# State-space layer on one core: ten products per half dealt otherwise between GpSimd and VectorE, and its steps placed anew

## The reference

```python
def _mamba(x, W_in, conv_w, conv_b, W_xproj, W_dt, b_dt, A_log, D_param, W_out):
    xp, z = jnp.split(x @ W_in.T, 2, axis=-1)              # 384 channels each
    xc = jax.nn.silu(causal_conv(xp, conv_w, 4 taps) + conv_b)
    dt, Bt, Ct = jnp.split(xc @ W_xproj.T, [12, 28], axis=-1)   # 16 states
    dt = jax.nn.softplus(dt @ W_dt.T + b_dt)
    A = -jnp.exp(A_log)
    def step(h, inp):
        dt_t, B_t, C_t, x_t = inp
        h = jnp.exp(dt_t[..., None] * A) * h + (dt_t * x_t)[..., None] * B_t[:, None, :]
        return h, jnp.einsum('bdn,bn->bd', h, C_t)
    y = scan(step) + xc * D_param
    return (y * jax.nn.silu(z)) @ W_out.T
h = h + 0.5 * (_mamba(ln(h)) + _mamba(ln(h)[:, ::-1])[:, ::-1])
```

## Time and profile before

| | before |
| --- | --- |
| median of 3 runs | 4684.36 us (4680.06 to 4692.94) |
| profiled execution | 4681.88 us, its span 4680.0 us |
| state-space scans | from 1221 to 3772 us of the span |
| busy share: TensorE, VectorE, GpSimd, ScalarE | 86%, 66%, 62%, 60% |

### The profile page before, as it was taken

The page is one execution under the profiler, slowest core; times in us unless marked ns, Lnnn a source line. Parts: engine busy times, 40 slices in busy tenths (PEclk is TensorE's granted clock), DMA queues, the critical chain, the costliest instruction groups (busy, mean ns, idle before and its releaser), DMA issues. The chain is left out here.

```text
span 4680.0 us, 76208 instructions
## 1 busy us (share of the span) xinstructions
PE 4045.9 (86%) x23616; PEld 2763.0 (59%) x23616; DVE 3086.8 (66%) x4728; ACT 2818.8 (60%) x4976; POOL 2901.5 (62%) x1573
## 2 busy tenths in 40 slices
PE   7999986997789988988998889889888766999994
PEld 4666654664456666666666666556565644666673
DVE  5766673111498888888888888888888875111114
ACT  3555542222688787888888887878788734121221
POOL 3222211442588888898988898888989841444441
PEclk9999996998899999999999999999999888999997
DMA  1000011343233333333333333333333321343456
GB/s 35 21 20 20 20 46 55 118 117 92 79 101 100 100 99 101 91 103 99 103 95 102 99 99 101 101 100 99 101 92 102 96 67 49 108 121 109 131 167 221
DMA packets 313323, 430.59 MB, mean 92 GB/s; under 512 B 44524, under 2 KB 181564, under 8 KB 312988
## 3 DMA queue, kind: packets, MB, share of 16 engines
q1 hardware_dynamic: 281856, 352.71, 25.6%
q0 software_dynamic: 28032, 73.17, 6.2%
q10 hardware_dynamic: 3100, 0.64, 0.1%
HBM read 359.42 MB, written 41.81 MB: 86 GB/s over the span
## 5 line engine op out<-in xcount | busy, mean ns | idle before, releaser
L1894 POOL TENSOR_TENSOR m_xh<-m_xh,m_Cb 128x1536 f32<-128x1536 f32 x320 | 1127.6, 3550 | 163.6 <-DVE m_xh L1877 163.2
L1903 POOL TENSOR_TENSOR m_xh<-m_u,m_Bb 128x1536 f32<-128x1536 f32 x320 | 1130.2, 3570 | 151.8 <-PE bank L1790 119.1
L1790 PE MATMUL bank<-ident,m_xh 128*128 128x128 f32 x6144 | 866.6, 283 | 59.2 <-issue 42.1
L1790 PEld LDWEIGHTS bank<-ident,m_xh 128*128 128x128 f32 x6144 | 728.6, 145 | 230.8 <-issue 204.8
L1877 DVE TENSOR_TENSOR_SCAN m_xh<-m_xh,bank 128x512 f32<-128x512 f32 x576 | 681.3, 1208 | 153.0 <-PE bank L1840 119.6
L1859 ACT ACTIVATE bank<-m_dt,m_Ac 128x512 f32<-128x512 f32 x960 | 635.1, 682 | 235.9 <-DVE m_xh L1887 154.2
L1877 DVE TENSOR_TENSOR_SCAN bank<-bank,m_xh 128x512 f32<-128x512 f32 x576 | 688.7, 1214 | 48.8 <-ACT bank L1859 46.7
L1877 DVE TENSOR_TENSOR_SCAN m_xh<-bank,m_xh 128x512 f32<-128x512 f32 x384 | 451.2, 1208 | 106.0 <-ACT bank L1859 98.6
L1840 PE MATMUL bank<-ident,m_uB 128*128 128x128 f32 x2304 | 375.5, 287 | 151.5 <-DVE m_xh L1887 100.5
L1204 ACT ACTIVATE f1t_h<-bank,f1t_b 128x512 f32<-128x512 f32 (+1 forms) x276 | 147.9, 587 | 509.7 <-PE bank L1234 509.7
L1831 ACT ACTIVATE m_uB<-m_uT,m_BT 128x384 f32<-128x384 f32 x768 | 407.7, 603 | 25.9 <-PE bank L1840 24.1
(11 more groups left out here) (381 smaller groups left out, 7047.6 us busy)
## 6 DMA issues: line engine op xcount, KB each, us to landing
m_Cb<-BC_rows SPq DMA_DIRECT2D x512, 256.0 KB, 3.4
m_Bb<-BC_rows SPq DMA_DIRECT2D x320, 256.0 KB, 4.2
f1t_w<-f_w SPq DMA_DIRECT2D x46, 576.0 KB
m_r<-m_dt POOLq DMA_DIRECT2D x32, 768.0 KB, 8.9
f1t_w1a<-f_w SPq DMA_DIRECT2D x46, 384.0 KB
f0t_w<-f_w SPq DMA_DIRECT2D x22, 576.0 KB
f1c_yg<-rows_y SPq DMA_DIRECT2D x16, 768.0 KB, 8.2
f1t_w1b<-f_w SPq DMA_DIRECT2D x92, 96.0 KB
```

Of the source, the lines that this page charges most:

```text
L1790: mm = pe.matmul(bank[:, c, sl], xh[n % NX][:, c, sl], K.ident[:, :], is_transpose=True, start=False, stop=(d == 1 and n == NS - 1), skip_ ...
L1894: pool.tensor_tensor(v, v, Cb[n % RC][:, :].unsqueeze(1).to_broadcast([P, DC, TOK]), ALU.mult).then_inc(s_prp, 1)
L1903: pool.tensor_tensor(xh[n % NX][:, :, :], u[d][:, :, :], Bb[k % RB][:, :].unsqueeze(1).to_broadcast([P, DC, TOK]), ALU.mult).then_inc(s_dB ...
```

## The change

Two tables change and nothing else: which states GpSimd reads out, and the positions of the steps.

In half 0 GpSimd reads out states 3, 11 and 15 in place of 4, 9 and 10; in half 1 states 1 and 15 in place of 0 and 9. The number stays ten a half, and VectorE's stays six. `BY_TURN` stays. In the diff the names ending in 0 or 1 belong to the preparation of half 0 or 1, which stands in the half before it; `pe_T`, `act_uB` and `pe_D` stand in their own half.

```diff
-            "pe_BT0": 17, "act_BT0": 19, "pe_BT1": 13, "act_BT1": 14, "act_uB0": (0, 10, 15, 21, 30, 35),
-            "act_uB1": (6, 9, 16, 20, 26, 36), "pe_T0": (6, 12, 18, 22, 30, 35), "pe_T1": (2, 6, 16, 24, 31, 35),
-            "pe_uT0": (36, 42, 46), "act_uT0": (38, 44, 47), "pe_uT1": (35, 39, 42), "act_uT1": (36, 41, 43), "y": (5, 6, 9),
-            "pe_yT": (8, 9, 11), "act_yT": (10, 11, 12), "pe_D0": (10, 12, 18), "pe_D1": (0, 6, 32), "pe_out": (15, 16),
-            "out": (15, 19), "act_rows": (8, 13), "rows": (8, 13), "stats": 15, "rstd": 17, "norm": 38, "pe_zT": (40, 47),
-            "act_zT": (42, 44), "pe_x0": (0, 1, 1), "act_x0": (0, 0, 2), "pe_conv0": (1, 1, 4), "act_conv0": (5, 7, 13),
-            "pe_conv1": (3, 3, 3), "act_conv1": (1, 3, 5), "pe_gate1": (23, 25, 28, 29), "act_gate1": (27, 29, 31, 33),
-            "pe_dt0": (18, 20, 21), "act_dt0": (21, 23, 24), "pe_dt1": (17, 21, 21), "act_dt1": (17, 23, 23), "pe_pj": (9, 9),
-            "act_pj": (16, 11), "act_xc": (14, 7), "act_e": (24, 25), "act_w1": (29, 26), "act_ln": (32, 31),
-            "pe_sp0": (34, 34, 40), "act_sp0": (36, 36, 42), "u0": (35, 35, 41), "pe_sp1": (33, 34, 37), "act_sp1": (34, 35, 40),
-            "u1": (34, 36, 39),
+            "pe_BT0": 17, "act_BT0": 20, "pe_BT1": 12, "act_BT1": 14, "act_uB0": (2, 10, 15, 21, 28, 33),
+            "act_uB1": (2, 9, 16, 20, 27, 34), "pe_T0": (7, 11, 17, 23, 30, 34), "pe_T1": (2, 6, 14, 24, 31, 35),
+            "pe_uT0": (37, 47, 47), "act_uT0": (40, 43, 44), "pe_uT1": (35, 36, 45), "act_uT1": (39, 40, 43), "y": (5, 6, 9),
+            "pe_yT": (7, 10, 13), "act_yT": (11, 13, 14), "pe_D0": (11, 14, 18), "pe_D1": (8, 16, 26), "pe_out": (15, 16),
+            "out": (16, 17), "act_rows": (9, 13), "rows": (9, 13), "stats": 18, "rstd": 27, "norm": 41, "pe_zT": (43, 47),
+            "act_zT": (43, 44), "pe_x0": (1, 1, 1), "act_x0": (0, 1, 3), "pe_conv0": (1, 1, 4), "act_conv0": (6, 8, 11),
+            "pe_conv1": (0, 0, 1), "act_conv1": (0, 4, 5), "pe_gate1": (23, 27, 27, 30), "act_gate1": (26, 29, 29, 33),
+            "pe_dt0": (19, 21, 21), "act_dt0": (23, 24, 24), "pe_dt1": (18, 19, 20), "act_dt1": (20, 21, 22), "pe_pj": (9, 9),
+            "act_pj": (17, 12), "act_xc": (14, 8), "act_e": (24, 24), "act_w1": (31, 27), "act_ln": (32, 32),
+            "pe_sp0": (33, 35, 42), "act_sp0": (37, 37, 41), "u0": (36, 39, 41), "pe_sp1": (32, 33, 40), "act_sp1": (34, 36, 41),
+            "u1": (35, 35, 41),
...
-        BY_POOL = (0, 2, 4, 5, 6, 8, 9, 10, 12, 14), (0, 2, 4, 5, 6, 8, 9, 10, 12, 14)
+        BY_POOL = (0, 2, 3, 5, 6, 8, 11, 12, 14, 15), (1, 2, 4, 5, 6, 8, 10, 12, 14, 15)
```

## The result

The changed kernel takes 4607.9 us (median of 4 runs, 4606.3 to 4615.3) against 4683.3 us for the kernel before. The ratio is 0.984, with a 95% interval of 0.982 to 0.986: faster by 75 us. The forecast was 4632, its range 4592 to 4702. The profiled execution of the changed kernel took 4615.3 us, its span 4612.5, so the traces differ by 67.5 us; the rest of the 75 lies in the spread of the runs, and what follows explains the 67.5.

A forecast was written before the change was run, and what follows sets the result against it. No single engine bounds it; the limit moves between TensorE, GpSimd and ScalarE. Terms 0.4 + 3.2 + 0 + 1.4 - 1.5 = 3.5 us a group, over 15 passages 52 us: 4632 us, range 4592 to 4702.

The forecast's parts named there:

- The signs named for it: Unit 30's wait under 1 us, unit 6's 1.5 to 3, projection 2 us sooner, a group of 156 to 158.
- new small waits: Gaps from gates and transposes at new positions and later bank release: 1.5 us a group lost, bounds 0 and 3.
- Unit 0 to 24 of half 0: Start of a group: first `y` needs the same convolutions and sums either way; +0.4 us, bounds -1.5 and +1.
- Unit 24 to unit 8 of half 1: From half 0 into half 1, paced by TensorE: its queue gets shorter, 3.2 us a group won.
- two sums, a D term, two waits: TensorE, unit 24 to unit 8 of half 1: savings of 1.0, 1.0 and 1.16 us, sum 3.2.
- The wait at 1796.03: TensorE's 0.58 us wait for VectorE's read-out of state 1: goes because GpSimd now reads that state.
- The wait at 1778.44: TensorE's 0.58 us wait that hangs on `zT`: loses its cause, moving with its step.
- Unit 8 to 33 of half 1: Stretch paced by ScalarE, with the same steps in the same sum: 0 us, bounds -1 and +0.5.
- Unit 33 to the next group: End of half 1, paced by GpSimd: one 3.5 us read-out less in its chain; +1.4 us, bounds -1 and +2.
- the gain is swallowed: Rival, chance 0.17: unit 30's waits go but ScalarE or TensorE is next late; 0.4 us a group, 4678 us.
- The read-out of state 11: Rival, chance 0.13: GpSimd's half 0 chain hangs on unit 35's scan, delaying read-out 12; 1.5 us a group lost, 4707 us.
- The clock rival: Rival, chance 0.05: TensorE's clock falls from 0.97 to 0.88 in half 0's second stretch, 4.0 us longer; 4744 us.

The follow-up runs named there:

- conv_back: The changed kernel with half 1's convolutions back at their old positions, behind the last sums: 4599.4 us, ratio to before 0.981.
- mend_d: The changed kernel with the first D term of half 0 at position 13 for 11, behind state 4's transposes: 4630.9 us, ratio to before 0.989.
- mend_conv: The changed kernel with ScalarE's first copy of a convolution in half 0 at position 2 for 0: 4610.3 us, ratio to before 0.984.
- mend_t8: The changed kernel with state 8's transposes in half 1 at position 22 for 24: 4595.6 us, ratio to before 0.980.
- places_only: The changed kernel's positions with the states dealt as before in both halves: 4719.3 us, ratio to before 1.007.
- half0_states: The changed kernel's positions, half 0's states dealt anew and half 1's as before: 4658.6 us, ratio to before 0.994.
- states_only: The kernel before with only the states dealt anew, all positions old: 4733.7 us, ratio to before 1.010.
- half1_states: The changed kernel's positions, half 1's states dealt anew and half 0's as before: 4653.1 us, ratio to before 0.993.
- dterm_back: The changed kernel with half 1's D terms back at positions 0, 6 and 32 for 8, 16 and 26: 4628.2 us, ratio to before 0.987.

## Why the prediction was right, and where it was not

The forecast was right in sign and nearly in size: 3.5 us a group for a measured 3.8 in the loop. The signs named for it came: 0.18 us before unit 30, 1.70 before unit 6 of half 1, the projection 3 us sooner after state 8's first transpose, a group of 156.4. That the sum is off by only 0.3 is partly luck. The first part came out 2.4 lower than forecast, and the reserve of 1.5 for new small waits and 0.5, 0.2 and 0.5 in the other parts made up for it. Nor did the sum foresee that either half of the change alone would cost time.

*Unit 0 to 24 of half 0: +0.4 forecast, -2.0 measured.* This step failed, and beyond its bound of -1.5. It held that the first `y` waits for the same work either way, which is so: `y` waits 0.18 for 0.80. But it looked at `y` alone, and it put TensorE's clock at nothing. ScalarE's first convolution copy now stands ahead of the decays of units 1 and 2, and the D term stands between state 4's transposes while it waits for ScalarE's copy of `yT`. TensorE in the changed kernel:

```profile
1705.27 0.66 PE L1840 MATMUL bank<-ident,m_uB 128*128 128x128 f32 x4 [1.41 <-ACT m_uB L1831]
...
1706.45 1.59 PE L1780 MATMUL bank<-m_dgD,m_xc 128*128 128x128 f32 x8 [0.53 <-ACT m_r L1803]
...
1708.69 1.06 PE L1840 MATMUL bank<-ident,m_uB 128*128 128x128 f32 x4
```

The state 4 transposes start at 1705.27, and the second set only at 1708.69. But the runs that undo one of these places each win back only 0.4 to 0.7 of the 2.0 us here (`conv_back`, `mend_d`, `mend_conv`). The rest goes with the clock: the lower level, 0.50, takes 5.5 us of this stretch on average, for 0.5 in the kernel before. `mend_d` shows its price within one execution, in the second and third group:

```profile
1529.60:1574.80 45.20, 42.34 (x223) 30.29 (x222) 37.71 (x48) 37.01 (x60) 34.33 (x11) 0.91 0.31 79
1689.50:1730.30 40.80, 37.94 (x221) 26.71 (x221) 37.33 (x47) 36.92 (x60) 34.24 (x11) 1.00 0.35 87
```

TensorE is idle for 2.86 us in both, so the whole difference of 4.4 us is busy time, in the group with the lower clock. The five groups of `mend_d` at 0.91 or 0.92 take 43.9 to 45.2 us, the six at 1.00 behind the loop's first 39.3 to 40.9. In `mend_t8`, whose half 0 is that of the changed kernel, the nine such groups take 38.4 to 40.3, and in the kernel before 38.6 to 40.9. So at a granted clock of 1.00 the new order costs nothing here, as far as `mend_t8` shows it; why the clock falls more often with it stays open. The 1.5 us set aside for "new small waits" were meant for such things; with them the forecast for this part would have been -1.1.

*Unit 24 to unit 8 of half 1: 3.2 forecast, 3.7 measured.* The size was right and the larger part of the reason wrong. I gave it to TensorE's queue: two sums, a D term, two waits. The D term is shown, at 0.95 us. The wait at 1796.03 is too: it is 0.59 us on average in `places_only` and `half0_states`, and gone with half 1's new states, and the stretch is then 0.6 and 0.5 us shorter (52.9 to 52.3, 50.2 to 49.8). The wait at 1778.44 is gone with the positions alone, but with these, two sums and D term included, the stretch wins only 0.5. The step that failed is the new deal of half 0, which I took for no gain by itself: it wins 2.5 to 2.7.

What the runs show in its place is this. VectorE's six read-outs of states 9 and 10 now stand in units 27 to 33, where it had waited 3.84 us for TensorE, and six fewer stand in units 33 to 47, where VectorE runs with hardly a wait: 21.5 us from unit 33 to the half's end, 23.9 before, and 25.2 with the positions alone. VectorE's idle time in the whole stretch fell from 7.6 us to 3.8, and only to 6.7 with the positions alone. The prediction had both facts, the later arrival at unit 30 and the shorter run at the end, but only as small terms of others. It also passed over a wait of TensorE for VectorE's read-out of state 11, before the third transpose of state 12: 0.64 us before, 1.21 with the positions alone, none once GpSimd reads out state 11. No run moves one state at a time, so how the 2.5 to 2.7 divide among states 3, 4, 9, 10, 11 and 15 is not shown.

It said that VectorE would next wait for TensorE at unit 6 of half 1, and it does (1.70 us, 1.75 before), so TensorE had to come sooner too. It did: from state 8's first transpose to the projection, 1728.32 to 1762.46, is 34.1 us, and it was 37.1. On average it is 34.2 for 36.5, 36.1 with the positions alone and 34.3 in `half0_states`, so this too came mostly with the deal of half 0:

```profile
1728.32 0.60 PE L1840 MATMUL bank<-ident,m_uB 128*128 128x128 f32 x4
...
1762.46 1.09 PE L1557 MATMUL bank<-m_zTa,m_win_a 128*128 128x512 f32 x2
```

*Unit 8 to 33 of half 1: 0 forecast, +0.2 measured.* ScalarE's chain held, also in every other kernel of the table: 40.1 to 41.7 us in all fourteen traces. Even where unit 24's wait went (`mend_t8`), the stretch came out at 40.2.

*Unit 33 to the next group: +1.4 forecast, +1.9 measured.* `states_only` shows it with the old positions (2.0). The reason holds: one large instruction less in GpSimd's chain. Counted from unit 33, the read-out of state 12 starts 12.1 to 12.4 us on in the kernel before, `places_only` and `half0_states`, and 10.2 to 10.5 in the changed kernel, `states_only` and `half1_states`.

*The size of the whole.* I multiplied by fifteen passages. Fourteen loop groups gave 53 us; groups 0 and 15 gave 11.7, where one passage had been counted (3.5). The mean wait at unit 0 of a loop group is 1.7 us in both kernels, and the first group has none; that this is why the written-out groups won more was only argued.

*The rivals.* That the gain is swallowed is what the unfitting halves of the change show. The read-out of state 11: its chain was as drawn, but the scan of unit 35 ended in time: read-out 12 started 28.2 us after state 8's first transpose (1756.49 from 1728.32), and 29.0 before. GpSimd idled 2.87 us ahead of read-out 11, a sign that I had named for this rival, and TensorE did not wait, which decides. The clock rival's sign came too, 0.92 in the first stretch of half 0, with 1.00 in the second: the clock fell where the time was lost, and the total was faster still. I had set that rival aside with a chance of 0.05 and kept the clock out of the sum; over a group the lower level (0.50) takes 12.7 us in the changed kernel, 10.0 before and 16.6 with the positions alone.

## What to carry to other kernels

When several engines are within a tenth of each other, an order is a fit and not a sum of edits: here positions alone cost 0.7%, the deal of read-outs alone 1.0%, and both together won 1.6%. Put an engine's optional work into the stretch where it waits and take it out of the stretch where it paces; to ask only whether a wait is removed misleads (3.84 us removed came back as 3.99 within three units). Before costing a wait's removal, list what comes second at that point: here it was only 0.5 us less late, and 3.3 of the 3.84 us stayed. And where TensorE paces, hold its idle time and its busy time apart: in one stretch 4.4 us between two groups were busy time at the lower clock (0.91 for 1.00), with the same idle time in both.

## What the runs showed of the hardware

Behind the loop's jump at the end of the fourth group TensorE idles 3.70 us and then runs at a granted clock of 0.50 for 6.1 us, to 1846.9. Of the thirteen jumps of the loop in the changed kernel's trace, with 2.9 to 3.7 us of idle time each, eight are followed within 6 us by 3.4 us at 0.50, three by 5.7 to 6.0, and two by none. Fifteen rows of two convolutions took 9.74 us there at a granted clock of 0.69, and as many of the same shape 6.73 at 1.00 in half 1 (the changed kernel):

```profile
1840.78 9.74 PE L1590 MATMUL bank<-m_xp,m_dg 128*128 128x512 f32 x15 [3.70 <-issue]
```

```profile
1768.75 6.73 PE L1590 MATMUL bank<-m_xp,m_dg 128*128 128x512 f32 x15
```

More surprising was that the clock also falls without such idle time ahead of it. In half 1 of the changed kernel TensorE goes from 1788 to 1807 with no gap above 0.14 us, on transposes, small projections and one D term:

```profile
1791.34 2.40 PE L1790 MATMUL bank<-ident,m_xh 128*128 128x128 f32 x20
...
1803.35 2.82 PE L1790 MATMUL bank<-ident,m_xh 128*128 128x128 f32 x12
...
1805.96 1.06 PE L1840 MATMUL bank<-ident,m_uB 128*128 128x128 f32 x4
```

Twenty at 1791.34 took 2.40 us, twelve at 1803.35 took 2.82: twice as long for each (0.24 us for 0.12). The granted clock is 1.00 from 1791 to 1800 and 0.50 from 1803 to 1809. It is behind part of the wait of 2.84 us at unit 24: the sixteen from 1803.35 to 1806.81 took 3.5 us, and at the earlier rate they would take 1.9, so an estimated 1.5 us of the wait is the clock. What makes it fall there is not shown: no run here changed the mix of transposes and other work alone. The nearest is `dterm_back`, which takes two of three D terms out of the stretch from unit 8 to 33 of half 1: the lower level (0.50) takes 9.0 us of it, for 4.1. But the kernel before has its D terms at the same places and spends 5.2 us there, so the places of the D terms alone don't explain it.
